# A filter layer with tokens on partitions, and another order in the experts' first pass

## The chip, the cores and the metric

One NeuronCore of a Trainium2 chip runs the whole kernel. It has five engines that work side by side: TensorE (PE; PEld are its weight loads), VectorE (DVE), ScalarE (ACT), GpSimd (POOL) and SyncE (SP), which only issues DMAs here. An engine works through its own instructions in order and waits on semaphores for the others. The metric is the device time of one execution in microseconds; lower is better.

## The reference

The input x has 2 sequences of 1024 tokens with 128 features, 2048 tokens in all, in f32. Four layers are added to it one after the other: A, F, B, F (A is a gated recurrent layer; the change does not touch it).

- B, the filter layer, on n = layernorm(x): q, k, v = n Wq', n Wk', n Wv'; each is Fourier transformed along its 128 features to 65 complex numbers; fq and fk are divided by (magnitude + 1e-8); fkv = running sum over the tokens of a sequence of fk * fv; the result is the inverse transform of fkv * conj(fq), and the layer returns n plus it. So x becomes x + n + values.
- F, on layernorm(x): causal attention with 16 heads, then four expert networks of which each token takes the best two by a softmax over four router logits. Expert 1 is silu(h W1) * (h W2), then a down product. Experts 0, 2 and 3 have one, three and two hidden layers with gelu. The first 32 output features of attention and experts are set to zero.

## The kernel before

X holds the tokens on partitions, as 16 tiles of 128 tokens by 128 features. Work goes in 4 chunks of 512 tokens (`NCH`, `TPC` = 4 tiles a chunk); chunks 0 and 1 are the first sequence. Every engine's program is written out by hand, and the order of a function's lines is the order on that engine's queue. PSUM is eight banks of 512 f32 (`PS`), handed out in turn by `Banks.take`; `psum_full` counts results written there, `psum_read` results copied away, and `all_read` waits for all.

**Filter layer (`b_tensor`, `b_scalar`, `b_vector`, `b_gpsimd`, lines 987 to 1162).** TensorE multiplies each of the three weights with the DFT table (L996); ScalarE copies the products to `bwf` (L1039), takes the root for the layernorm and copies the transposed normed tokens to HT (L465). Then `spectra(c)` makes, for a chunk, spectra with frequencies on 65 partitions and 512 tokens along the row (L1006): real and imaginary part of q, k, v, six banks. ScalarE squares q and k out of PSUM (L1045), copies all three (L1052), and takes the root of the squares' sums (L421). VectorE sums the squares (L1068), adds epsilon (L1074), takes the reciprocal (L1075) and scales q and k by it (L1079): this is `unit(c)`. GpSimd multiplies k and v (`b_times`, L1131 to L1133). VectorE makes the running sums along the row with two scans a chunk (L1090), the second half of a sequence carrying on from the first. GpSimd multiplies by conj(q) (`b_unbind`, L1144 to L1148). TensorE transforms back (L1018), which puts tokens on partitions again; VectorE adds it to X (`add`, L1097) and takes the layernorm's statistics for the next layer (`stats`, L410 and L413). For the last chunk VectorE does `b_times` and `b_unbind` itself. The first transposes and four QKV products (L447) of the next F layer stand between the last `output` calls on TensorE.

**Experts (end of `f_tensor`, `f_scalar`, `f_vector`).** When a sequence's last heads are added up (`heads_added`), TensorE projects its attention output (`proj`, L1333), VectorE joins it to XL (`join`), and the normed result is transposed to HT. The first pass is expert 1: two `up` products a chunk (L1386), `silu(c)` on ScalarE (L1544), `gate(c)` on VectorE (L1732), and `down1(c)` (L1407), whose result VectorE adds with the token's weight (`add1`, L1770). The weights come from the router product (L1440, 32 records of 4 columns), a softmax and a chain of small comparisons on VectorE (L1741 to L1765). The second pass goes over the chunks with experts 0, 2 and 3: `up`, `mid` (L1397), `down` (L1417), gelu on ScalarE (L1562). `down1(c)` for c of 2 and 3 waits until `add1(c-2)` has freed its bank. Chunks 0 and 1 of the first pass start while the second sequence's projection is still outstanding.

**Weights.** `w_sync` on SP's queue, in layer A, loads the weights of B and F with eleven DMAs; `W_LOADED` is the count that their users wait for.

Of the kernel before, what the change touches and what calls it, by code (L numbers as in the profile page):

```python
# [16 lines left out]
P = 128  # L17
B, S, D = 2, 1024, 128
NT = B * S
# [73 lines left out]
def hybrid_kernel(nc, x, a_w, a_wab, a_small, a_conv, a_bog, a_bout, a_wout, b_w, b_dft, b_idft,  # L93
                  f_w, f_n, f_qk, f_mid, f_down, f_wo, f_rows, eye, causal, out):
    ctx = ExitStack()
    with ctx:
# [108 lines left out]
        with ExitStack() as sw:  # L205
# [3 lines left out]
            bidft = sb("bidft", [P, 2, D], at=sw, side="right")  # L209
            bwf = sb("bwf", [P, 3, 2, NB], at=sw, side="right")  # L210
# [13 lines left out]
            with ExitStack() as sB:  # L224
                QF = {i: sb(f"QF{i}", [P, 3, 2, CH], at=sB) for i in (1, 2, 0)}
                KV = [sb(f"KV{i}", [P, 4, CH], at=sB) for i in range(2)]
                SQF = sb("SQF", [P, 2, 2, CH], at=sB)
                mag = [sb(f"mag{i}", [P, 2, CH], at=sB) for i in range(2)]
                PRB = sb("PRB", [P, 4, CH], at=sB)
                CUM = sb("CUM", [P, 2, B, S], at=sB)  # L230
                YF = sb("YF", [P, 2, NT], at=sB)
# [94 lines left out]
        sums_ready = sem("sums_ready")  # L326
# [660 lines left out]
        B_RES = 3 + NCH + 3 * NCH  # L987
        OUT_BANKS = 6

        def b_tensor(pe, banks, nth):  # L990
            base = banks.n
            pe.wait_ge(w_loaded, W_LOADED)
            pe.wait_ge(x_ready, nth)
            for n in range(3):
                k = banks.take()
                pe.matmul(PS[:, k, 0:2 * NB], bw[:, n, :], bdft[:].rearrange("p r f -> p (r f)"),  # L996
                          start=True, stop=True).then_inc(psum_full, 1)
            pe_transpose_in(pe, banks, XL, FIRST_NORM[nth])
            banks.all_read()

            def spectra(c):
                for n in range(3):
                    if c:
                        pe.wait_ge(psum_read, banks.n - 2)
                    for r in range(2):
                        last = pe.matmul(PS[0:NB, 2 * n + r, :], bwf[:, n, r, :], HT[:, c * CH:(c + 1) * CH],  # L1006
                                         start=True, stop=True)
                    last.then_inc(psum_full, 1)
                    banks.n += 1

            def output(c):
                pe.wait_ge(y_ready, c + 1)
                if c >= 2:
                    pe.wait_ge(values_added, c - 1)
                for i in range(TPC):
                    t = (c * TPC + i) * P
                    for r in range(2):
                        last = pe.matmul(PS[:, OUT_BANKS + c % 2, i * P:(i + 1) * P], YF[0:NB, r, t:t + P],  # L1018
                                         bidft[0:NB, r, :], start=(r == 0), stop=(r == 1))
# [4 lines left out]
            for c in range(NCH // B):  # L1024
                output(c)
            assert banks.n == base + B_RES
            banks.all_read()
            for g in range(NCH // B):
                pe.wait_ge(values_added, g + 1)
                pe_transpose_x(pe, banks, g)  # L1030
            output(NCH - 2)
            for t in range(TPC):
                pe_qkv(pe, banks, FIRST_RESULT[nth + 1], t)
            output(NCH - 1)

        def b_scalar(act, link, ask, reads):
            for n in range(3):
                k = reads.next()
                act.activation(bwf[:, n].rearrange("p r f -> p (r f)"), PS[:, k, 0:2 * NB],  # L1039
                               ACT.Copy).then_inc(psum_read, 1)  # L1040
            act_sqrt(act, ask, stat[:])
            act_ht(act, reads)
            for c in range(NCH):
                act.wait_ge(psum_full, reads.n + 2)
                act.activation(SQF[0:NB], PS[0:NB, 0:4, :].rearrange("p (n r) t -> p n r t", n=2),  # L1045
                               ACT.Square).then_inc(squares_ready, 1)
                if c >= 3:
                    act_sqrt(act, ask, mag[c % 2][0:NB])
                    act.wait_ge(y_ready, c - 2)
                for n in range(3):  # L1050
                    reads.next()
                    act.activation(QF[c % 3][0:NB, n], PS[0:NB, 2 * n:2 * n + 2, :], ACT.Copy).then_inc(psum_read, 1)  # L1052
# [881 lines left out]
```

## Time and profile before

| | us |
|---|---|
| median of 3 runs (1143.45 to 1147.26) | 1146.95 |
| the profiled execution | 1147.34 |
| its span, first to last instruction | 1145.5 |
| busy: PE, DVE, ACT, POOL | 678.0, 830.2, 534.1, 328.0 |

The mean granted clock of TensorE is 0.775 of full speed (1.0 is 2.4 GHz, 0.5 is 1.2 GHz). Busy shares are means over layers with different limits, so a layer is read by itself: first a row of its stretch with each engine's busy time, then the chain of work that ended last in it, then the groups and the single instructions. In such rows x is the number of instructions, and brackets give the idle time before an instruction and what ended it. Times are us from the span's start unless marked ns; a matmul record is one pass, and an f32 product leaves two.

### The profile page before, as it was taken

The page shows a single profiled execution, that of the slowest core. Times are in us where ns is not written, and L with a number is a line of the kernel's source. Part 1 is how long each engine was busy: PE and PEld are TensorE (multiplying, and loading weights), DVE is VectorE, ACT ScalarE, POOL GpSimd, SP SyncE. Part 2 cuts the span into 40 slices and gives each one's busy share as a digit, 9 for nine tenths or more (in the row PEclk, how much of TensorE's full clock was granted, in tenths as well). Part 3 has the DMA queues.
Part 4 walks back from the last instruction along what each step waited for, and adds up shares of the span by engine and source line. Part 5 has one row for each costly group of instructions (what it writes and reads, how often), then busy time and mean ns, then how long its engine had stood idle before and what let it go on. Part 6 is the DMA issues. An engine that isn't in the chain of part 4 may idle for free.

```text
span 1145.5 us, 11993 instructions
## 1 busy us (share of the span) xinstructions
PE 678.0 (59%) x4000; PEld 327.8 (29%) x4000; DVE 830.2 (72%) x1478; ACT 534.1 (47%) x882; POOL 328.0 (29%) x290
## 2 busy tenths in 40 slices
PE   3993004000004007598888889873275988879998
PEld 1452004000003005222222556530251222225555
DVE  5899999888889997966586523359989665865212
ACT  2414003333331004699998322252146999983222
POOL 1050652000003303257655000006812576550000
PEclk9985555555555557599999889977575999998999
DMA  3150048400000010541010000000005311100000
GB/s 96 60 157 4 3 101 180 132 19 19 0 19 19 0 27 10 178 130 57 29 57 1 1 1 1 1 1 0 0 1 185 122 57 31 55 1 1 1 19 19
DMA packets 37253, 51.30 MB, mean 45 GB/s; under 512 B 5128, under 2 KB 27016, under 8 KB 36168
## 3 DMA queue, kind: packets, MB, share of 16 engines
q1 hardware_dynamic: 36424, 49.76, 15.8%
q10 hardware_dynamic: 768, 0.79, 0.4%
q8 instruction: 32, 0.52, 0.2%
q14 instruction: 29, 0.24, 0.1%
HBM read 21.02 MB, written 16.92 MB: 33 GB/s over the span
## 4 chain that ended last, share of the span: by engine, by line
DVE 44%; PE 24%; POOL 11%; ACT 9%; issue 8%; DMA 2%; SPq 1%; ACTq 1%; DVEq 0%; POOLq 0%
POOL PX L1284 10%; PE PS L1397 6%; ACT PX L1537 6%; PE PS L1386 5%; PE PS L1417 4%; DVE S L847 4%; DVE D L843 4%; DVE P L844 3%; DVE P L840 3%; DVE mag L1075 2%; PE PS L1372 2%; DVE RP L862 2%; DVE PRR L861 2%; DVE CUM L1090 1%; PE PS L1407 1%
## 5 line engine op out<-in xcount | busy, mean ns | idle before, releaser
L1537 ACT ACTIVATE PX<-PS 128x1024 f32<-128x1024 f32 (+1 forms) x320 | 270.9, 975 | 13.3 <-PE PS L1352 12.9
L1284 POOL TENSOR_TENSOR PX<-PX,maskf 128x256 f32<-128x256 f32 (+1 forms) x192 | 178.0, 961 | 118.1 <-ACT PX L1537 118.1
L1372 PE MATMUL PS<-PX,VA 128*32 128x512 f32 (+3 forms) x1536 | 166.7, 505 | 27.8 <-POOL PX L1284 18.2
L1770 DVE SCALAR_TENSOR_TENSOR X<-PS,wts,X 128x96 f32<-128x96 f32 x128 | 38.4, 315 | 121.0 <-PE PS L1417 103.9
L1352 PE MATMUL PS<-QS,KS 64*128 64x512 bf16 (+3 forms) x768 | 105.5, 339 | 7.5 <-ACT PX L1537 4.4
L1709 DVE RECIPROCAL DEN<-DEN 128x512 f32<-128x512 f32 x32 | 107.3, 3353 | 1.1
L611 PE MATMUL PS<-fw,ones 128*128 128x384 f32 x2 | 1.6, 928 | 160.1 <-DVE fw L1567 160.1
L718 ACT ACTIVATE P<-S,AC 128x16 f32<-128x16 f32 x128 | 41.2, 322 | 114.4 <-DVE S L847 114.4
L983 POOL TENSOR_TENSOR PRQ<-PA,LQK 128x2048 f32<-128x2048 f32 (+7 forms) x8 | 20.8, 2616 | 200.4 <-DMA WS<-S 183.2
L1386 PE MATMUL PS<-HT,fw 128*128 128x512 f32 x144 | 72.8, 656 | 1.5 <-DVE HG L1732 1.0
L1352 PEld LDWEIGHTS PS<-QS,KS 64*128 64x128 bf16 x768 | 30.1, 94 | 140.7 <-ACT PX L1537 83.5
L606 PE MATMUL PS<-ones,HT 64*128 64x1 f32 x64 | 13.0, 348 | 90.4 <-ACT HT L702 90.4
L1372 PEld LDWEIGHTS PS<-PX,VA 128*32 128x32 f32 x1536 | 33.0, 108 | 81.4 <-ACT PX L1537 53.3
L1131 POOL TENSOR_TENSOR KV<-QF 65x1024 f32<-65x1024 f32 x3 | 9.1, 3041 | 161.3 <-DVE QF L1079 159.0
L1707 DVE LOAD_MASK_SELECT DEN<-PS x32 | 0.4, 14 | 73.0 <-PE PS L1372 71.5
L465 ACT ACTIVATE HT<-PS 128x512 f32<-128x512 f32 x24 | 13.8, 600 | 79.1 <-PE PS L438 57.1
L611 PEld LDWEIGHTS PS<-fw,ones 128*128 128x128 f32 x2 | 0.5, 310 | 160.2 <-DVE fw L1567 160.2
L843 DVE TENSOR_REDUCE D<-P 128x16 f32<-128x144 f32 x128 | 38.8, 303 | 5.2 <-ACT P L711 0.7
L847 DVE TENSOR_REDUCE S<-P 128x16 f32<-128x144 f32 x128 | 38.8, 303 | 4.6 <-DVE P L844 0.2
L586 PE MATMUL PS<-HT,CWT 128*128 128x512 f32 (+3 forms) x96 | 41.4, 593 | 0.0
L840 DVE TENSOR_TENSOR P<-W,S 128x128 f32<-128x128 f32 x128 | 37.3, 292 | 4.6
L629 PE MATMUL PS<-awout,RT 128*128 128x128 f32 x32 | 6.6, 402 | 57.4 <-DMA RT<-RO 57.4
(276 smaller groups left out, 1532.9 us busy)
## 6 DMA issues: line engine op xcount, KB each, us to landing
QS<-qs_d SPq DMA_DIRECT2D x64, 98.0 KB
qs_d<-QP SPq DMA_DIRECT2D x24, 256.0 KB, 3.6
ks_d<-QP SPq DMA_DIRECT2D x24, 256.0 KB, 3.9
KS<-ks_d SPq DMA_DIRECT2D x64, 96.0 KB
K<-LQK SPq DMA_DIRECT2D x16, 256.0 KB
W<-WS SPq DMA_DIRECT2D x16, 256.0 KB, 4.4
qkv_d<-CY SPq DMA_DIRECT2D x3, 1024.0 KB, 4.0
LQK<-qkv_d SPq DMA_DIRECT2D x8, 256.0 KB, 4.9
```

The source lines that it names most:

```text
L586: last = pe.matmul(PS[:, k, skip:CH], CWT[:, 4 * n + j, :], HT[:, t + skip - back:t + CH - back], start=(j == 3), stop=True, skip_group_ch ...
L840: link(v.tensor_tensor(P1[:, n % 2, :, :, 0:HD], bcast(W2[:, g, cs], 1, 2), bcast(S2[:, n], 2, C), ALU.mult))
L843: link(v.tensor_reduce(D2[:, g, :, cs], P1[:, n % 2], AX.X, ALU.add))
L847: v.tensor_reduce(S2[:, n + 1], P2[:], AX.X, ALU.add).then_inc(chunk_done, 1)
L1284: pool.tensor_tensor(block, block, bcast(maskf[:], 1, 2 * halves), ALU.mult).then_inc(probs_masked, 1)
L1352: last = pe.matmul(PS[:, 2 * (u % DEPTH) + side, at:at + CH - c0], KS[b][rows, pair, kt * P:(kt + 1) * P], QS[b][rows, pair, qc * CH + c0: ...
L1372: last = pe.matmul(PS[32 * h:32 * h + 32, SCORES_BANKS + qc, c0:CH], VA[b][:, kt, h, :], px[:, i % 2, at:at + CH - c0], start=(kt == 0), s ...
L1386: last = pe.matmul(PS[:, bank + m, :], fw[:, col + m * P:col + (m + 1) * P], rhs(c), start=True, stop=True)
L1397: last = pe.matmul(PS[:, bank + m, :], fmid[:, w + k, m * P:(m + 1) * P], h, start=(k == 0), stop=(k == len(parts) - 1))
L1417: last = pe.matmul(PS[:, 6 + t % 2, j * OUTC:(j + 1) * OUTC], h[:, m, t * P:(t + 1) * P], fdown[:, e, m, :], start=(m == 0), stop=(m == 1))
L1537: act.activation(tile(PX[u % PDEPTH][:]), tile(PS[:, k:k + 2, :]), ACT.Exp).then_inc(probs_ready, 1)
L1709: v.reciprocal(DEN[:], DEN[:]).then_inc(den_ready, 1)
```

## The change

**Filter layer.** Tokens now stay on the partitions. `bwf` becomes one row of 3x2x65 columns, and `spectra(c)` takes HT's tile as the stationary side and `bwf` as the moving one: per tile of 128 tokens 390 numbers, in banks 4 to 7, handed over two tiles at a time. The frequencies are stored rotated by one, so that frequency 0 comes last. ScalarE squares and copies by pairs of tiles. The running sum becomes TensorE products (`sums`): a triangular matrix (`maskf`) for the tile itself, a matrix of ones for the tiles before it in the chunk, and `LAST`, which picks the last token's row, for the carry from the chunk before. ScalarE copies the sums (`CUM`), in its program ahead of the root of the chunk two later. `b_unbind` makes products only; `turn` transposes and adds them with products against identity and minus identity (`NIDENT`), ScalarE copies the result, and `output` is one product a tile, since its 128 rows now hold the 65 real and 63 imaginary parts. Buffers are one per chunk, with fewer waits between chunks. VectorE writes three constant tiles into SQ. The weights-by-DFT products wait for the first F layer's last expert addition in place of the layer's statistics; `bidft` is loaded by three DMAs. For the last chunk VectorE unbinds straight from PSUM and copies the turned tile.

**Experts, both F layers.** `up(0, 2)` and `up(1, 0)` go ahead of the wait for the last heads and the projections of chunks 2 and 3. The ups of chunks 2 and 3 go ahead of the router's product, `silu(2)` and `silu(3)` ahead of the router's exponential, `gate(2)` and `gate(3)` ahead of the router's work on VectorE. `down1(2)` and `down1(3)` go behind the last `mid` of the second pass's chunk 0.

```diff
-        B_RES = 3 + NCH + 3 * NCH
-        OUT_BANKS = 6
+        B_RES = 3 + NCH + 2 * NCH
+        SPEC_BANK, SUM_BANK, TURN_BANK = 4, 0, 2
+        OUT_BANK = (3, 7, 3, 3)
...
-            pe.wait_ge(x_ready, nth)
+            pe.wait_ge(down_read, 2 * TILES)
             for n in range(3):
                 k = banks.take()
                 pe.matmul(PS[:, k, 0:2 * NB], bw[:, n, :], bdft[:].rearrange("p r f -> p (r f)"),
                           start=True, stop=True).then_inc(psum_full, 1)
+            pe.wait_ge(x_ready, nth)
             pe_transpose_in(pe, banks, XL, FIRST_NORM[nth])
-            banks.all_read()
...
+                for p in range(2):
+                    pe.wait_ge(psum_read, banks.n - 1 if c else base + 3 + 1)
+                    for i in range(2 * p, 2 * p + 2):
+                        t = (c * TPC + i) * P
+                        last = pe.matmul(PS[:, SPEC_BANK + i, 0:3 * 2 * NB], HT[:, t:t + P], bwf[:],
                                          start=True, stop=True)
                     last.then_inc(psum_full, 1)
...
+            def sums(c):
+
+                pe.wait_ge(kv_ready, c + 1)
+                pe.wait_ge(sums_read, c)
+                carry = c % (S // CH) > 0
+                for i in range(0, TPC, 2):
+                    two, second = SUMS_PS[:, i:i + 2], SUMS_PS[:, i + 1]
+                    if carry:
+                        pe.matmul(two, LAST, bcast(CUM[c - 1][:, TPC - 1], 1, 2), start=True, stop=False,
+                                  skip_group_check=True)
+                    for j in range(i):
+                        pe.matmul(two, ONES, bcast(KV[c][:, j], 1, 2), start=(j == 0 and not carry), stop=False,
+                                  skip_group_check=True)
+                    pe.matmul(two, maskf[:], KV[c][:, i:i + 2], start=(i == 0 and not carry), stop=False,
+                              skip_group_check=True)
+                    last = pe.matmul(second, ONES, KV[c][:, i], start=False, stop=True, skip_group_check=True)
+                last.then_inc(sums_full, 1)
+
+            def turn(c):
+
+                pe.wait_ge(y_ready, c + 1)
+                pe.wait_ge(turned_ready, c)
+                for i in range(TPC):
+                    at = slice(i * P, (i + 1) * P)
+                    pe.matmul(PS[:, TURN_BANK, at], ABF[c][:, 0, i, 0:P], ident[:], start=True, stop=False,
+                              skip_group_check=True)
+                    pe.matmul(PS[0:P // 2, TURN_BANK, at], ABF[c][:, 1, i, 0:P // 2], ident[:], start=False, stop=True,
+                              skip_group_check=True)
+                    last = pe.matmul(PS[P // 2:P, TURN_BANK, at], ABF[c][:, 1, i, P // 2:P], NIDENT, start=False,
+                                     stop=True, skip_group_check=True)
+                last.then_inc(turned_full, 1)
...
+            sums(0)
+            sums(1)
+            turn(0)
+            output(0)
+            sums(2)
+            turn(1)
             banks.all_read()
+            output(1)
+            sums(3)
+            turn(2)
             for g in range(NCH // B):
                 pe.wait_ge(values_added, g + 1)
                 pe_transpose_x(pe, banks, g)
-            output(NCH - 2)
+            output(2)
+            turn(3)
             for t in range(TPC):
                 pe_qkv(pe, banks, FIRST_RESULT[nth + 1], t)
-            output(NCH - 1)
+            output(3)
...
             for c in range(NCH):
...
+                spectra(c)
+                if c >= 2:
+                    sums(c - 2)
+                act_sqrt(act, ask, mag[c][:])
+            turned(0)
+            sums(2)
+            turned(1)
+            turned(2)
...
+        def b_times(eng, link, c):
+
+            k = QKF[c][:].rearrange("p (t n) r f -> p t n r f", n=2)[:, :, 1]
+            w, to = VF[c], TKV[c]
+            out = KV[c][:].rearrange("p t (r f) -> p t r f", r=2)
+            link.open(eng.tensor_tensor(to[:, 0], k, w[:], ALU.mult))
+            link.open(eng.tensor_tensor(to[:, 1, :, 0], k[:, :, 0], w[:, :, 1], ALU.mult))
+            link(eng.tensor_tensor(to[:, 1, :, 1], k[:, :, 1], w[:, :, 0], ALU.mult))
+            eng.tensor_tensor(out[:, :, 0], to[:, 0, :, 0], to[:, 0, :, 1], ALU.subtract)
+            if c == NCH - 1:
+                eng.wait_ge(kv_ready, NCH - 1)
+            eng.tensor_tensor(out[:, :, 1], to[:, 1, :, 0], to[:, 1, :, 1], ALU.add).then_inc(kv_ready, 1)
...
             pe.wait_ge(psum_read, banks.n - 1)
             up(0, 0, F_E1A)
             banks.all_read()
+            up(0, 2, F_E1B)
+            pe.wait_ge(up_read, hidden + 1)
+            up(1, 0, F_E1A)
             pe.wait_ge(heads_added, (rep * B + 2) * (NG - 1) * 2)
             for c in range(NCH // B, NCH):
                 proj(c, HT_BANKS + c - NCH // B)
-            up(0, 2, F_E1B)
-            pe.wait_ge(up_read, hidden + 1)
-            up(1, 0, F_E1A)
             pe.wait_ge(h1_ready, gated + 1)
             up(1, 2, F_E1B)
             down1(0)
             pe_transpose_in(pe, banks, SQ, FIRST_NORM[nth], range(NCH // B, NCH), HT_BANKS - NCH // B)
             down1(1)
             banks.all_read()
+            for c in range(NCH // B, NCH):
+                pe.wait_ge(up_read, hidden + c)
+                up(c, 0, F_E1A)
+                pe.wait_ge(h1_ready, gated + c)
+                up(c, 2, F_E1B)
...
                 mid(4, 2, [HB[:, k, :] for k in range(2)])
+                if c == 0:
+                    down1(NCH - 2)
+                    down1(NCH - 1)
...
-            for dst, src in ((bw, b_w), (bdft, b_dft), (bidft, b_idft), (fw, f_w), (fn, f_n), (fmid, f_mid),
+            for dst, src in ((bidft[0:NB - 1], b_idft[1:NB, 0]), (bidft[NB - 1:NB], b_idft[0:1, 0]),
+                             (bidft[NB:P], b_idft[1:P - NB + 1, 1])):
+                sp.dma_start(dst, src).then_inc(w_loaded, 16)
...
+            silu(2)
+            silu(3)
             ask.wait()
             act.activation(pr[:], lg[:], ACT.Exp).then_inc(to_dve, 1)
-            silu(2)
-            silu(3)
...
             v.tensor_tensor(X[:], X[:], XL[:], ALU.add).then_inc(x_sum, 1)
+            gate(2)
+            gate(3)
```

## Rows read from the trace of the kernel before

**Rows 1.** Stretches of the filter layer: length, busy us by engine (records), clock, DMA.
```profile
766.70:820.90 54.20, 18.77 (x46) 7.57 (x44) 53.92 (x20) 16.87 (x15) 35.54 (x19) 0.68 0.00 0
820.90:848.40 27.50, 15.79 (x68) 13.11 (x68) 24.38 (x43) 4.75 (x11) 11.06 (x6) 0.57 0.00 0
```

**Rows 2.** Stretches of the first expert layer, same view.
```profile
647.40:657.40 10.00, 10.00 (x17) 3.83 (x16) 5.05 (x24) 4.24 (x5) 0.00 (x0) 0.71 0.00 1
657.40:665.10 7.70, 3.50 (x17) 3.51 (x17) 5.65 (x24) 0.63 (x1) 0.00 (x0) 0.68 0.01 2
...
680.70:743.70 63.00, 60.79 (x283) 38.72 (x281) 19.00 (x72) 17.85 (x19) 0.00 (x0) 1.00 0.00 1
```

**Rows 3.** Chain of waits, filter layer: shares by engine, tile, line.
```profile
by line: DVE mag L1075 25.1%; DVE CUM L1090 15.6%; DVE QF L1079 10.0%; issue 6.4%; PE PS L1006 5.1%; DVE mag L1074 4.3%; DVE XL L417 4.0%; PE PS L447 3.6%; PE PS L1018 3.3%; ACT QF L1052 2.6%; DVE mag L1068 2.4%; PE PS L432 1.9%; ACT SQF L1
```

**Rows 4.** Line L1709: count, ns min/median/max, first and last start, form.
```profile
L1709 DVE RECIPROCAL DEN<-DEN x32: 3352/3353/3354, 491.5 to 1026.0; 128x512 f32<-128x512 f32 x32
```

**Rows 5.** Groups in the filter layer by form: busy us, mean ns, idle before.
```profile
L1075 DVE RECIPROCAL mag<-mag 65x1024 f32<-65x1024 f32 x4 | 26.2, 6549 | 0.1
...
L465 ACT ACTIVATE HT<-PS 128x512 f32<-128x512 f32 x7 | 4.2, 598 | 36.9 <-PE PS L438 32.1 <-PE PS L432 4.8
...
L1097 DVE TENSOR_TENSOR X<-X,PS 128x512 f32<-128x512 f32 x4 | 2.7, 666 | 0.0
...
L1144 DVE TENSOR_TENSOR PRB<-CUM,QF 65x1024 f32<-65x1024 f32 x1 | 1.2, 1222 | 0.0
```

**Rows 6.** Timeline of the filter layer: start, us, engine, line, [idle before].
```profile
745.22 1.42 PE L996 MATMUL PS<-bdft,bw 128*128 128x130 f32 x6 [2.57 <-issue]
...
763.90 5.37 PE L1006 MATMUL PS<-HT,bwf 128*65 128x512 f32 x12 [1.16 <-ACT QF L1052]
...
777.30 0.68 DVE L1074 TENSOR_SCALAR mag<-mag 65x1024 f32<-65x1024 f32 x1
...
780.15 1.27 POOL L1132 TENSOR_TENSOR KV<-QF 65x512 f32<-65x512 f32 x1
...
791.26 2.17 POOL L1132 TENSOR_TENSOR KV<-QF 65x512 f32<-65x512 f32 x1
792.30 1.68 DVE L1074 TENSOR_SCALAR mag<-mag 65x1024 f32<-65x1024 f32 x1
...
837.29 3.62 PE L1018 MATMUL PS<-bidft,YF 65*128 65x128 f32 x16
...
845.14 1.95 PE L1018 MATMUL PS<-bidft,YF 65*128 65x128 f32 x16
```

**Rows 7.** Line L1567, columns as in rows 4.
```profile
L1567 DVE TENSOR_SCALAR fw<-fw,fn x1: 412/412/412, 358.1 to 358.1; 128x384 f32<-128x384 f32 x1
```

**Rows 8.** Timeline of the first expert layer, columns as in rows 6.
```profile
630.67 2.00 PE L1333 MATMUL PS<-fwo,AO 128*128 128x96 f32 x16 [2.32 <-DVE AO L1715]
...
635.89 1.22 DVE L1732 TENSOR_TENSOR HG<-HS,PS 128x1024 f32<-128x1024 f32 x1
...
643.38 4.06 PE L1440 MATMUL PS<-fw,HT 128*128 128x4 f32 x32
...
647.30 10.12 PE L1386 MATMUL PS<-HT,fw 128*128 128x512 f32 x16
...
661.62 3.70 PE L1407 MATMUL PS<-fdown,HG 128*128 128x96 f32 x16 [4.20 <-DVE X L1770]
```

**Rows 9.** Stretches cut finer, for the granted clock, same view as rows 1.
```profile
788.00:804.00 16.00, 0.56 (x2) 0.56 (x3) 15.93 (x7) 2.31 (x3) 15.20 (x8) 0.56 0.00 0
...
844.00:848.00 4.00, 3.53 (x24) 2.77 (x22) 1.74 (x3) 2.13 (x6) 0.00 (x0) 0.95 0.00 0
...
660.00:664.00 4.00, 2.38 (x11) 2.41 (x12) 3.43 (x11) 0.00 (x0) 0.00 (x0) 0.52 0.00 0
1031.00:1036.00 5.00, 5.00 (x20) 3.67 (x21) 2.81 (x4) 0.00 (x0) 0.00 (x0) 0.66 0.01 3
```

**Rows 10.** Stretch of the second expert layer, same view as rows 1.
```profile
1064.30:1080.20 15.90, 15.90 (x49) 8.16 (x48) 1.98 (x8) 4.58 (x5) 0.00 (x0) 0.94 0.00 1
```

More of the change, by code:

```diff
@@ L1011, in output @@
             def output(c):
-                pe.wait_ge(y_ready, c + 1)
+                pe.wait_ge(turned_ready, c + 1)
                 if c >= 2:
-                    pe.wait_ge(values_added, c - 1)
+                    pe.wait_ge(values_added, 1 if c == 2 else c)
                 for i in range(TPC):
[L1016 to L1019, printed above, removed]
+                    at = slice(i * P, (i + 1) * P)
+                    last = pe.matmul(PS[:, OUT_BANK[c], at], YT[c][:, at], bidft[:], start=True, stop=True)
@@ L1023, in b_tensor @@
                 spectra(c)
-            for c in range(NCH // B):
-                output(c)
             assert banks.n == base + B_RES
+            pe.wait_ge(consts_ready, 1)
+            sums(0)
[4 more added lines that the diff above has]
+            turn(1)
             banks.all_read()
+            output(1)
+            sums(3)
+            turn(2)
             for g in range(NCH // B):
@@ new lines, in sums, with turned @@
+            def sums(c):
+                act.wait_ge(sums_full, c + 1)
+                act.activation(CUM[c][:], SUMS_PS, ACT.Copy).then_inc(sums_read, 1)
+            def turned(c):
+                act.wait_ge(turned_full, c + 1)
+                act.activation(YT[c][:], PS[:, TURN_BANK, :], ACT.Copy).then_inc(turned_ready, 1)
+            for c in range(NCH):
+                spectra(c)
+                if c >= 2:
+                    sums(c - 2)
+                act_sqrt(act, ask, mag[c][:])
@@ L1104, in b_vector @@
             sum_squares(0)
-            unit(0)
-            for c in range(1, NCH):
+            for c in range(NCH):
                 unit(c)
-                sums(c - 1)
-                if c >= 3:
-                    add(c - 3)
-                    stats(c - 3)
             v.wait_ge(unit_ready, NCH)
-            v.wait_ge(sums_ready, NCH - 2)
-            link(b_times(v, NCH - 1))
-            sums(NCH - 1)
-            add(NCH - 3)
-            stats(NCH - 3)
-            b_unbind(v, link, NCH - 1)
@@ new lines, in b_unbind @@
+        def b_unbind(eng, c, sums):
+            q = QKF[c][:].rearrange("p (t n) r f -> p t n r f", n=2)[:, :, 0]
+            z = sums.rearrange("p t (r f) -> p t r f", r=2)
+            to = ABF[c][:].rearrange("p w t (r f) -> p w t r f", r=2)
+            eng.tensor_tensor(to[:, 0], z, bcast(q[:, :, 0], 2, 2), ALU.mult)
+            eng.tensor_tensor(to[:, 1, :, 0], z[:, :, 1], q[:, :, 1], ALU.mult)
+            eng.tensor_tensor(to[:, 1, :, 1], z[:, :, 0], q[:, :, 1], ALU.mult).then_inc(y_ready, 1)
@@ L1443, in f_tensor @@
             assert banks.n == base + F_RES
-            for c in range(NCH // B, NCH):
-                pe.wait_ge(up_read, hidden + c)
-                up(c, 0, F_E1A)
-                pe.wait_ge(h1_ready, gated + c)
-                up(c, 2, F_E1B)
-            down1(NCH - 2)
             pe.wait_ge(up_read, hidden + NCH)
@@ L1752, in f_vector @@
             for i in range(E4):
-                if i == 2:
-                    gate(2)
                 for j in range(i):
@@ L1778, in add1 @@
                     add_expert(c * TPC + t, 1, PS[:, 6 + c % 2, t * OUTC:(t + 1) * OUTC]).then_inc(down_read, 1)
-            add1(0)
-            gate(3)
-            for c in range(1, NCH):
+            for c in range(NCH):
                 add1(c)
```

151 lines of the change are left out of this document (70 added, 81 removed).

## The prediction

> **What bounds the kernel now.** I read the stages first: each row is one stretch's length, busy time by engine and granted clock. In the filter layer's loop, 54.2 us, VectorE is busy 53.92 and TensorE 18.77; in its last 27.5 us VectorE 24.38 [rows 1]. The layer runs from the last expert addition, 743.7, to its own last addition, 848.4: 104.7 us. In the experts [rows 2] TensorE has the most work, but does 10.00 us of first-pass products at a clock of 0.71 and is busy only 3.50 of the 7.70 us behind them. From 680.7 on it is busy 60.79 of 63.0; that stretch is at its bound and the change leaves it alone. The chain of waits in the filter layer [rows 3] says what ends last: reciprocals 25.1%, scans 15.6% (16 us), scaling of q and k 10.0%, all VectorE. Groups and timeline give prices and order.
>
> The profiled execution took 1147.34 us, span 1145.5; the median of the runs is 1146.95. I sum against 1147.3, 0.03% off.
>
> **The filter layer, price by price.** The spectra go from 65 partitions to 128: a chunk of 512 tokens becomes 4 tiles by 130 numbers for each of q, k, v.
>
> VectorE. Reciprocal: 520 in a row instead of 1024. 512 cost 3.353 [rows 4], 1024 cost 6.549 [rows 5], so 520 cost 3.40; 3.15 saved, four times. Squares' sum: 520, by L1097's 512 in 0.67, so 0.68. Scaling: 1040, by L1144's 1024 in 1.22, so 1.24 [rows 5]. Epsilon: half of L1074's 0.68, so 0.4. The scans go to TensorE. While GpSimd works the short steps stretch: L1074 took 1.68 beside L1132's 2.17, 0.68 alone [rows 6]. I take 1.35 times; the ends 1.0 and 1.7 are worth 2.6 us less and 2.6 more over the layer.
>
> GpSimd. Products of a chunk: 520 + 4x260 numbers; L1132's 512 took 1.27 alone, 2.17 beside VectorE [rows 6], so 1.3 + 4x0.7 = 4.1 to 7; I take 5.0. Unbinding, 520 + 2x260: 2.75.
>
> ScalarE. Two squares of 520, two pairs of copies, a root; by L465's 512 in 0.60 [rows 5] 0.61 each and 0.9 a pair, 3.6 a chunk, below VectorE's 6.2.
>
> TensorE. Each f32 product leaves two records. One of 128 columns takes 0.122 us at the high clock, 0.23 at the low (L1018: 16 in 1.95 and 3.62); one of 512 takes 0.45 (L1006: 12 in 5.37) [rows 6]. So at the high clock spectra, 390 columns, are 1.3 per two tiles; sums, four products of 260 and two of 130, 2.2, with a carry two more of 260, 3.1; turning, 24 records, 2.9; output, 8 records, 1.0. All nearly double at the low clock.
>
> **Schedule at these prices.** *Front.* The weights-by-DFT products wait for the last expert addition, 743.75, and no longer for the statistics: L996 starts 1.4 us earlier than 745.22 [rows 6]. Two tiles instead of a chunk suffice for the first square. First reciprocal 762.3, not 767.4: 5.1 saved. *Loop.* Four units of epsilon 0.54, reciprocal 3.40, squares' sum 0.75, scaling 1.6 make 24.5 us. A wait is added: ScalarE copies chunk c-2's sums ahead of chunk c's root, so behind it are queued root 2 and with it all of VectorE's unit 2. Sums 0 need GpSimd's products of chunk 0 (773.2) and TensorE past its last spectra (772.0). I expect some 8 us at the low clock here, as TensorE has 2.6 us of work in each 6; sums 0 end 777.6, root 2 at 778.9, and VectorE, free at 774.6, loses 4.3. Loop ends 791.0, not 820.9: 24.8 more saved. *Tail.* Sums 2 from 790.4 to 792.6, copy, turn 1 to 796.1, copy, output 1 to 797.8, sums 3 to 800.9, turn 2 to 803.9, transposes of two chunks 1.3, output 2 to 806.3, turn 3 to 809.2, four QKV tiles (384 columns each) to 811.8, their copies and the squares' sums of q and k, together 3.6 by estimate and in the old tail too, last addition 816.1. That is 25.1 against 27.5: 2.4 saved, TensorE-bound where VectorE and GpSimd were. Together 848.4 - 816.1 = 32.3; what follows hangs on this addition as before.
>
> The three constant tiles (about 0.7 of VectorE) lie under the first spectra. bidft's load becomes three DMAs ahead of the other weights, two issues more on SP; the first weight is used at 358.1 [rows 7], some 150 us after its issue, so even 10 us would be covered.
>
> **The experts, price by price.** Now TensorE idles 2.3 us for the last heads, then projects at 630.67 and goes on with up products; gate 0 runs at 635.89 [rows 8]. After: two up products (3.5) go ahead of that wait, fill it, and push the projections to 631.85. Joins, squares and gate 0 behind them come 1.2 later (gate 0 ends 638.3), and TensorE, with nothing left, idles 633.7 to 638.3. The idle 4.2 before L1407 at 661.62 was followed by a clock of 0.52 [rows 8, 9], so a fall here is likely (1.9 lost). Then nothing interrupts: up 1.75, down 1.9, transposes 1.05, down 1.9, four ups 7.0, to 651.9 (653.8 with the fall). Router 3.95 by L1440, its read 0.5, second pass from 656.4 (658.3) instead of 665.1. Now the 16 records after the router take 10.12 us [rows 8] where the high clock needs 7; that low stretch moves onto the second pass, 2.5 lost again (1.7 to 3.4). The gap of 4.2 goes, and so does L1407's low-clock 3.70. Inside the second pass's chunk 0 two down products (3.6) replace one. The choice of experts, some 38 VectorE steps of about 0.2, 6.8 us by estimate, ends near 665; the down products that need its additions come at 672. That hides it; with the cover gone each late us is a us. Chunk 1 starts 675.3 (677.2), not 680.7: 5.4 (3.5) saved. In the second expert layer the projections begin at 1031.0 and chunk 1 at 1080.2 [rows 9, 10], 49.2 against 50.0, so 4.5 (2.7). Together 6.2 to 9.9; I take 7.5.
>
> **Sum:** 1147.3 - 32.3 - 7.5 = 1107.5.
>
> **Rivals.** *Low clock through the filter layer.* TensorE's work comes in pieces between waits; from 788 to 804 the clock was 0.56 [rows 9], and the L1018 burst at 837 still ran low [rows 6]. Low from 765 to 800 the addition ends at 823, total 1114; low to the end, 30 us of TensorE's tail become 60 and it ends at 844, total 1135. Against: from 784 on TensorE has work almost without a gap, and the burst from 836 on had brought 0.95 by 844 to 848 [rows 9]. The Trainium skill (TensorE: Matmul & The Clock Gate, "A second HAM failure mode: psum-queue depth-cycling") has such micro-idles make the clock oscillate, which would be this rival; no run of this order shows it yet.
> *VectorE held by GpSimd.* If each of eight short steps in units 1 to 3 waited out a whole GpSimd instruction of 1.3, they would lose 10.4 instead of 2.6: 1115; half of one on average, 1110. For: L1074, issued at 792.30, ends at 793.98, about its lone 0.68 after L1132 ended at 793.43. Against: the reciprocal kept its 6.55 throughout, and it is over half of a unit, so many steps will meet a GpSimd engine between instructions. The Trainium skill (SBUF — State Buffer, "Who interferes with whom") makes it an exclusive lock for the whole instruction; the row agrees.
> *High clock and no contention:* addition at 810, experts 10: 1099.
> *The experts give nothing:* pause at 633.7 and the moved low stretch eat it all: 1115.
> *Slower: weight loads not hidden.* Sums, turns and outputs have 184 records, each with a 128-wide load. L1407's records, 96 columns, took 0.23 each at the low clock, so a load costs no more. Were each to stand before its stream, 42 us come on top of 60, addition at 886, total 1177; it decides once the tail needs over 72 us. Against: L1018 gets through load and stream of 128 columns in that same 0.23.
>
> **How the numbers follow.** Forecast 0.54; low clock 0.14; VectorE held 0.10; high clock 0.10; experts nothing 0.08; slower 0.03; saved so little that it can't be told 0.01. Under 0.5%, 5.7 us, can't be told from no change. The filter layer's 25 to 37 and the experts' 2 to 12 give 1098 to 1120; with part of the low-clock case 1096 to 1123. Faster 0.95 (all but the last two, less a hundredth for a low clock with more against it), same 0.02, slower 0.03.
>
> **What would show it.** Right: reciprocals near 3.4; root 2 waiting for sums 0; some 72 us from the experts' last addition to the filter layer's; a pause of 4 to 5 us before gate 0 and none before chunk 2's down products. Wrong: a clock near 0.5 after 790, short VectorE steps over twice their lone price, a second pass that still waits at its start, or attention stretches that change.

## The result and the profile after

The changed kernel took 1100.18 us (median; 1098.63 to 1102.87) against 1145.20 (1142.39 to 1147.26) for the kernel before, run beside it: ratio 0.9612, 95% interval 0.9592 to 0.9632. Its profiled execution took 1101.15, span 1099.0: 46.5 less span than before. I forecast 1107.5.

I take the account between marks that both traces have. From the last head addition of attention to the last expert addition: 113.2 before, 109.3 after in the first expert layer, 3.9 saved. From there to the filter layer's last addition: 104.7 and 65.2, 39.5 saved. From the second attention's last head addition to the end of the span: 114.65 and 112.27, 2.4 saved. From the filter layer's last addition to the first exponential of the next attention it is 32.7 before and 32.9 after. What is left, 0.7, lies in stretches that the change does not touch.

Stretches of the changed kernel: the filter layer's loop and its tail, then the first expert layer up to its second chunk, and the rest of it (length, busy us of TensorE, its weight loads, VectorE, ScalarE, GpSimd with records; granted clock; DMA).

```profile
754.90:781.80 26.90, 20.25 (x92) 14.15 (x91) 22.29 (x16) 11.36 (x24) 16.45 (x21) 0.94 0.00 1
781.80:803.70 21.90, 19.36 (x135) 14.15 (x133) 13.39 (x40) 6.21 (x14) 3.12 (x3) 1.00 0.00 1
629.20:636.70 7.50, 3.04 (x19) 2.16 (x18) 4.90 (x8) 2.51 (x3) 0.00 (x0) 0.83 0.01 2
636.70:645.00 8.30, 8.26 (x45) 6.19 (x45) 4.75 (x4) 1.99 (x3) 0.00 (x0) 0.75 0.00 0
645.00:656.60 11.60, 11.27 (x50) 7.35 (x48) 2.70 (x4) 3.71 (x4) 0.00 (x0) 0.91 0.00 0
656.60:675.60 19.00, 18.92 (x63) 10.38 (x64) 9.20 (x48) 7.14 (x8) 0.00 (x0) 0.87 0.00 1
675.60:738.50 62.90, 60.71 (x283) 38.66 (x282) 19.96 (x76) 16.81 (x18) 0.00 (x0) 1.00 0.00 1
```

Against [rows 1]: the loop is 26.9 where it was 54.2, VectorE no longer fills it (22.29), and TensorE works 20.25 in it. In the tail TensorE is busy 19.36 of 21.9 at the high level (1.00) where the old tail had 0.57. Against [rows 2]: the 62.9 us at the end of the experts stand as they were; the gain lies ahead of them.

The chain of waits in the filter layer, shares by line:

```profile
by line: DVE mag L1148 10.5%; PE PS L1047 9.0%; PE PS L1049 8.7%; DVE XL L426 6.4%; PE PS L1018 5.7%; PE PS L1034 5.0%; PE PS L1061 4.9%; PE PS L1036 4.7%; PE PS L1031 3.8%; DVE QKF L1152 3.5%; issue 3.1%; PE PS L441 3.0%; PE PS L1038 2.4%;
```

In [rows 3] three VectorE lines led it. Now the reciprocal is 10.5%, and of the next eight lines seven are TensorE: the layer has changed its bound. In order of time the chain still runs through VectorE's first two units up to 766, then through GpSimd's products of chunk 1 to 770, and from there through TensorE and the copies that it waits for. How much each part of the new layer brings is read from this; no run takes one part alone.

Groups of the layer (busy us, mean ns) and its timeline (start, us, engine, line, idle before):

```profile
L1148 DVE RECIPROCAL mag<-mag 128x520 f32<-128x520 f32 x4 | 13.6, 3402 | 0.1
...
L1152 DVE TENSOR_TENSOR QKF<-QKF,mag 128x1040 f32<-128x1040 f32 x4 | 4.9, 1236 | 0.0
```

```profile
752.42 0.70 DVE L1141 TENSOR_TENSOR mag<-SQF 128x520 f32<-128x520 f32 x1 [3.39 <-ACT SQF L1100]
...
754.95 3.40 DVE L1148 RECIPROCAL mag<-mag 128x520 f32<-128x520 f32 x1
...
765.31 1.04 PE L1034 MATMUL PS<-KV,SQ 128*128 128x260 f32 x4
...
768.21 0.64 DVE L1147 TENSOR_SCALAR mag<-mag 128x520 f32<-128x520 f32 x1 [2.23 <-ACT mag L430]
...
770.03 0.71 PE L1031 MATMUL PS<-CUM,SQ 128*128 128x260 f32 x2 [3.01 <-POOL KV L1196]
...
772.69 1.70 PE L1034 MATMUL PS<-KV,SQ 128*128 128x260 f32 x4
...
776.25 0.79 DVE L1147 TENSOR_SCALAR mag<-mag 128x520 f32<-128x520 f32 x1 [2.07 <-ACT mag L430]
...
780.52 1.24 DVE L1152 TENSOR_TENSOR QKF<-QKF,mag 128x1040 f32<-128x1040 f32 x1
...
797.78 2.85 PE L456 MATMUL PS<-fw,HT 128*128 128x384 f32 x8
...
803.04 0.68 DVE L1157 TENSOR_TENSOR X<-X,PS 128x512 f32<-128x512 f32 x1
```

The reciprocal measures the 3.40 that [rows 4, 5] gave. VectorE waits twice for a root that stands behind a copy of sums, as forecast for one of them. Four records of 260 columns (two products) cost 1.04 at 765.31 and 1.70 at 772.69, behind TensorE's wait of 3.01. The granted clock by stretches of 4 us, around this wait and at the start of the experts' second pass:

```profile
766.00:770.00 4.00, 1.02 (x6) 0.73 (x4) 1.75 (x2) 2.95 (x7) 3.85 (x6) 1.00 0.02 6
770.00:774.00 4.00, 3.97 (x12) 3.24 (x13) 3.96 (x3) 0.72 (x2) 2.43 (x3) 0.58 0.00 0
774.00:778.00 4.00, 4.00 (x30) 2.68 (x28) 1.89 (x3) 1.13 (x2) 3.66 (x5) 1.00 0.00 0
...
655.00:659.00 4.00, 3.59 (x9) 2.36 (x10) 2.09 (x12) 1.54 (x2) 0.00 (x0) 0.50 0.01 2
```

In this execution the clock is high while TensorE waits, low when it starts again, and high 4 us on.

TensorE's timeline in the first expert layer after, with the gate that it waits for:

```profile
635.47 1.22 DVE L1793 TENSOR_TENSOR HG<-HS,PS 128x1024 f32<-128x1024 f32 x1
...
636.74 3.78 PE L1447 MATMUL PS<-HT,fw 128*128 128x512 f32 x4 [4.50 <-DVE HG L1793]
640.31 2.21 PE L1468 MATMUL PS<-fdown,HG 128*128 128x96 f32 x16
...
644.99 7.06 PE L1447 MATMUL PS<-HT,fw 128*128 128x512 f32 x16
651.89 4.39 PE L1506 MATMUL PS<-fw,HT 128*128 128x4 f32 x32
656.68 6.86 PE L1447 MATMUL PS<-HT,fw 128*128 128x512 f32 x10 [0.41 <-DVE lg L1804]
```

The wait of 4.20 of [rows 8] is gone; one of 4.50 has come ahead of gate 0, with four records at 3.78 behind it, which take 1.98 at the high clock (the same four in two of the runs below). The ten records after the router take 6.86; ten of the 16 in 7.06 are 4.4.

### The profile page after: what moved, and what is told of

Read it like the earlier page. It is cut to its first block, busy times and chain, and to the rows that moved or that the text cites. A ratio compares the mean times of both kernels' runs of the same rounds, so it can differ in the third digit from the quotient of the medians.

```text
span 1099.0 us, 12216 instructions
## 1 busy us (share of the span) xinstructions
PE 672.6 (61%) x4104; PEld 331.8 (30%) x4104; DVE 788.6 (72%) x1474; ACT 527.7 (48%) x899; POOL 299.6 (27%) x290
## 4 chain that ended last, share of the span: by engine, by line
DVE 39%; PE 28%; POOL 12%; ACT 8%; issue 8%; DMA 3%; SPq 2%; ACTq 1%; DVEq 0%; POOLq 0%
POOL PX L1345 11%; PE PS L1447 7%; PE PS L1458 6%; ACT PX L1598 6%; PE PS L1478 4%; DVE D L852 4%; DVE S L856 4%; DVE P L853 4%; DVE P L849 3%; PE PS L1433 2%; DVE RP L871 2%; DVE PRR L870 2%; PE PS L1468 1%; PE PS L1413 1%; SPq L1274 1%
## 5 line engine op out<-in xcount | busy, mean ns | idle before, releaser
L1433 PEld LDWEIGHTS PS<-PX,VA 128*32 128x32 f32 x1536 | 32.9, 108 | 80.2 <-ACT PX L1598 53.4
L1447 PEld LDWEIGHTS PS<-HT,fw 128*128 128x128 f32 x144 | 29.6, 212 | 45.1 <-issue 31.4
L1190 POOL TENSOR_TENSOR TKV<-QKF,VF 128x520 f32<-128x520 f32 x3 | 3.7, 1233 | 141.3 <-DVE QKF L1152 141.3
```

The costliest lines, as they stand in the source:

```text
L1433: last = pe.matmul(PS[32 * h:32 * h + 32, SCORES_BANKS + qc, c0:CH], VA[b][:, kt, h, :], px[:, i % 2, at:at + CH - c0], start=(kt == 0), s ...
L1447: last = pe.matmul(PS[:, bank + m, :], fw[:, col + m * P:col + (m + 1) * P], rhs(c), start=True, stop=True)
```

## The experiments

**The changed kernel again**, no edit, beside the next two.

> The changed kernel once more, as a base for the runs beside it. Both theories: about 1100 us, 0.961 of the kernel before.

1101.06 (1098.76 to 1103.12), ratio 0.9614 [0.9593, 0.9635]. Its stretches repeat: 109.8, 64.9, 112.5. One thing differs: sums 1 start 30.0 us after the last expert addition and take 6.1 until the first turning starts, where the first profile has 31.5 and 4.9, so the clock is low there for longer:

```profile
770.00:774.00 4.00, 4.00 (x10) 3.26 (x11) 3.97 (x3) 0.66 (x2) 2.37 (x3) 0.50 0.00 0
774.00:778.00 4.00, 4.00 (x23) 2.88 (x23) 0.71 (x2) 1.13 (x2) 3.72 (x6) 0.76 0.00 0
```

The layer ends at the same place either way, but a run with an edit must be held against the profile with the same low stretch.

**Each half alone.** The filter layer with the experts' old order, and the reverse (all functions of the filter layer as before):

```diff
-            for c in range(NCH // B, NCH):
-                pe.wait_ge(up_read, hidden + c)
-                up(c, 0, F_E1A)
-                pe.wait_ge(h1_ready, gated + c)
-                up(c, 2, F_E1B)
...
             last.then_inc(psum_full, 1)
...
+            for c in range(NCH // B, NCH):
+                pe.wait_ge(up_read, hidden + c)
+                up(c, 0, F_E1A)
+                pe.wait_ge(h1_ready, gated + c)
+                up(c, 2, F_E1B)
+            down1(NCH - 2)
```

```diff
-                        last = pe.matmul(PS[:, SPEC_BANK + i, 0:3 * 2 * NB], HT[:, t:t + P], bwf[:],
...
+                        last = pe.matmul(PS[0:NB, 2 * n + r, :], bwf[:, n, r, :], HT[:, c * CH:(c + 1) * CH],
```

> The filter layer's part alone, the experts as before. Theory, by the two traces: the layer went from 104.7 to 65.2 us (743.71 to 848.4 and 738.53 to 803.7), so 39.5 of the gain are its own and this takes about 1106. Rival, that the two parts need each other (the clock that the experts leave behind, buffers): the filter part alone gives 32 or less, the 32.3 of the forecast, and this takes 1113 or more.

> The experts' new order alone, the filter layer as before. Theory, by the two traces: from the last heads to chunk 1 of the second pass 50.2 became 46.4 in the first expert layer and 49.3 about 47 in the second, so 6 us: about 1139. Rival, that the pause before gate 0 and the moved low clock eat it: within 2 us of 1145. Forecast's middle: 7.5, about 1138.

filter_only: 1106.96 (1106.43 to 1107.16), ratio 0.9665 [0.9649, 0.9682]; filter layer 64.9, first experts 113.2 as before. experts_only: 1139.28 (1136.31 to 1142.03), ratio 0.9955 [0.9937, 0.9972]; 109.8 and 104.7. Alone they save 38.0 and 5.7 against their runs of before (1145.0), 43.8 in sum; together they save 43.9 against the same runs. They add; neither needs the other.

**Which of the new order's moves costs?** Chunk 0's second pair and chunk 1's first pair of products behind the projections again, the rest of the change kept:

```diff
-            up(0, 2, F_E1B)
-            pe.wait_ge(up_read, hidden + 1)
-            up(1, 0, F_E1A)
...
+            up(0, 2, F_E1B)
+            pe.wait_ge(up_read, hidden + 1)
+            up(1, 0, F_E1A)
             pe.wait_ge(h1_ready, gated + 1)
```

> The changed kernel with the two up products back behind the projections; the rest of the experts' new order stays. Theory (the pause costs): gate 0 comes 1.2 us earlier, TensorE's wait for it shrinks from 4.5 to about 1 us, the low clock behind it (two products in 3.78 where 1.75 is the full price) goes: 2 to 3 us saved per expert layer, 4 to 6 in all, about 1095. Rival (what is ahead is won): the 3.5 us of up products are back on the path, 2 to 3 us lost per layer, about 1105.

1094.52 (1094.36 to 1096.51), ratio 0.9564 [0.9547, 0.9581]: 6.5 below after_again. Putting products ahead of the projections, which I had priced as filling the wait, lost 3 us in each layer: the stretches are 106.4 and 108.9, where the changed kernel has 109.3 and 112.3. TensorE's timeline in the first layer:

```profile
629.58 2.79 PE L1394 MATMUL PS<-fwo,AO 128*128 128x96 f32 x16 [2.32 <-DVE AO L1776]
632.16 4.53 PE L1447 MATMUL PS<-HT,fw 128*128 128x512 f32 x8
636.87 1.98 PE L1447 MATMUL PS<-HT,fw 128*128 128x512 f32 x4 [0.17 <-DVE HG L1793]
...
654.75 6.07 PE L1447 MATMUL PS<-HT,fw 128*128 128x512 f32 x10 [0.41 <-DVE lg L1804]
```

The heads' wait of 2.32 is back, but the 4.50 ahead of gate 0 is 0.17, and the records behind it are at 1.98. They hardly start earlier, though: 7.4 us after the last head addition, against 7.5 in the changed kernel, because the projections (2.79) and the eight records (4.53) ran low. In the second layer these took 2.00 and 3.62 behind the same wait, and the start is at 6.6. So in the first layer all that was gained is clock, not the earlier gate that the theory named.

**One pair ahead, one behind**, the split of the two:

```diff
             up(0, 2, F_E1B)
-            pe.wait_ge(up_read, hidden + 1)
-            up(1, 0, F_E1A)
...
+            pe.wait_ge(up_read, hidden + 1)
+            up(1, 0, F_E1A)
```

> The changed kernel with one up product (chunk 0's second) ahead of the wait for the last heads and the other behind the projections. Theory: it fills the 2.3 us in which TensorE waited for the heads without pushing the projections back, gate 0 stays at its early place and the wait for it is still covered by the other product: about 1094.5, as with both behind, or 1 to 2 us less. Rival (any product ahead delays gate 0): between 1095 and 1100.

1092.95 (1089.48 to 1094.51), ratio 0.9544 [0.9521, 0.9567]. In its profile the first expert layer took 103.2, the second stretch 108.8; the profiled execution was the fastest of its four (1089.48), so these two are its best and not its middle.

**Is it the clock and not the wait?** Four products of no use (8 records) between the projections and the wait for gate 0; order as in the change:

```diff
+            for i in range(4):
+                pe.matmul(PS[:, 7, :], fw[:, 0:P], HT[:, 0:CH], start=True, stop=True)
             pe.wait_ge(h1_ready, gated + 1)
```

> The changed kernel, with four products of 512 columns put on TensorE behind the projections whose results nobody reads (bank 7, overwritten later), so that it works through 3.5 of the 4.5 us in which it waits for gate 0. Theory (the low clock after the pause is part of the cost): the two products behind gate 0 take 2.0 and not 3.8, 1.5 to 2 us saved per expert layer, 3 to 4 in all, about 1097. Rival (only the late gate 0 costs, the clock is hidden): within 1 us of 1100.

1092.61 (1089.52 to 1093.06), ratio 0.9539 [0.9518, 0.9560]: 7.6 below the changed kernel's 1100.18, more than was expected. TensorE's timeline in the first layer, and one line of the second:

```profile
637.99 1.98 PE L1447 MATMUL PS<-HT,fw 128*128 128x512 f32 x4 [1.03 <-DVE HG L1795]
...
651.10 3.63 PE L1508 MATMUL PS<-fw,HT 128*128 128x4 f32 x32
655.13 4.53 PE L1447 MATMUL PS<-HT,fw 128*128 128x512 f32 x10 [0.41 <-DVE lg L1806]
...
1006.93 6.23 PE L1447 MATMUL PS<-HT,fw 128*128 128x512 f32 x10 [0.41 <-DVE lg L1806]
```

The added 3.6 us lie in the wait. Behind it 1.98 stands for 3.78, and, unforeseen, the router takes 3.63, not 4.39, and the second pass's start 4.53, not 6.86; in the second layer it takes 6.23, not 7.31. The records behind gate 0 start 7.51 after the last head addition, to the hundredth as in the changed kernel: gate 0 is no earlier, only the clock differs. Work that computes nothing saved 7.6 us, so the low clock was the loss.

**The router in two lots among the pass**, so that no 32 small records stand in a row:

```diff
                 up(c, 0, F_E1A)
+                last = router(range((c - 2) * TB, (c - 1) * TB))
                 pe.wait_ge(h1_ready, gated + c)
                 up(c, 2, F_E1B)
...
-            for t in range(TILES):
-                last = pe.matmul(PS[:, ROUTER_BANK, t * E4:(t + 1) * E4], HT[:, t * P:(t + 1) * P],
```

> The changed kernel with the router's 32 small records split in two and put between the up products of chunks 2 and 3, instead of in one piece behind them; nothing else. Theory (the router's piece is what lets the clock fall at the start of the second pass, 6.86 us for 10 records where 4.5 is the full price, and leaves a wait of 0.4): 2 to 2.8 us saved per layer, 4 to 5.5 in all, about 1095.5. Rival (the fall comes from the pause before gate 0 and the low stretch behind it, or moves to another place): within 1.5 us of 1100.

1095.48 (1094.31 to 1099.30), ratio 0.9567 [0.9540, 0.9593]. The ten records take 4.53 in both layers (and in both of best and best2 below, which have the router in lots too; behind the router in one piece they take 4.53 only in the first layer of one_ahead and of filler, and 6 us or more in every other profile). The wait ahead of them grew from 0.41 to 1.59, since on VectorE the read now stands behind a gate; the 3.78 after gate 0 stays. Its slowest run reaches into the changed kernel's range.

**Is the wait for the root on the path?** A chunk's root ahead of the copy of sums on ScalarE:

```diff
                 spectra(c)
+                act_sqrt(act, ask, mag[c][:])
                 if c >= 2:
                     sums(c - 2)
-                act_sqrt(act, ask, mag[c][:])
```

> The changed kernel, with ScalarE taking the root of chunk c before it copies the sums of chunk c-2. VectorE's two waits of 2.2 and 2.1 us before units 2 and 3 go. Theory (the layer is bound by TensorE from the sums of chunk 1 on, 770 to 798, and by unit 1 and GpSimd's products before them): at most 1 us saved, 1099 to 1101. Rival (VectorE's loop still sets the end, as the forecast had it): 4 us saved, about 1096.

1103.17 (1099.52 to 1103.81), ratio 0.9631 [0.9609, 0.9653]. VectorE's last scaling there:

```profile
777.91 1.36 DVE L1152 TENSOR_TENSOR QKF<-QKF,mag 128x1040 f32<-128x1040 f32 x1
```

It ends 38.4 after the last expert addition (740.86) instead of 43.2, and the layer still takes 65.0; after_again, with the same start (30.0) and length (6.1) of sums 1, takes 64.9. Nearly 5 us taken from VectorE's loop are worth nothing: its end is off the path. The total is 2 to 3 us above the changed kernel's and not within the forecast 1099 to 1101; no stretch that the edit touches shows a loss.

**Half of the turning left out**, two of three products a tile:

```diff
-                    pe.matmul(PS[0:P // 2, TURN_BANK, at], ABF[c][:, 1, i, 0:P // 2], ident[:], start=False, stop=True,
...
-                    last = pe.matmul(PS[P // 2:P, TURN_BANK, at], ABF[c][:, 1, i, P // 2:P], NIDENT, start=False,
...
```

> The changed kernel without the second half of the turning (the two 64-row products a tile against identity and minus identity are left out, so the imaginary parts' share of the values is missing). They take 0.35 us a tile on TensorE, 1.4 a chunk. Theory (TensorE bounds the layer's second half): 4 to 5.6 us saved, about 1095.5. Rival (copies, GpSimd and VectorE are next and hide it): under 2 us, 1098 or more.

1100.03 (1092.07 to 1100.60), ratio 0.9596 [0.9569, 0.9622]: the total did not fall. The layer takes 62.7, 2.3 to 2.5 less where 4 to 5.6 were expected. Its clock, and TensorE at sums 3:

```profile
770.00:774.00 4.00, 3.83 (x10) 3.17 (x11) 3.96 (x3) 0.86 (x3) 2.57 (x4) 0.50 0.00 0
...
786.00:790.00 4.00, 2.62 (x7) 2.24 (x8) 2.48 (x5) 0.00 (x0) 0.23 (x1) 0.54 0.00 0
790.00:794.00 4.00, 4.00 (x16) 3.26 (x16) 0.43 (x1) 0.00 (x0) 0.00 (x0) 0.61 0.00 0
```

```profile
787.38 1.24 PE L1031 MATMUL PS<-CUM,SQ 128*128 128x260 f32 x2 [3.12 <-DVE KV L1191]
```

The first low stretch stands ahead of any turning and is that of after_again (sums 1 take 6.1). With less to do TensorE then waits 3.12 ahead of sums 3 for VectorE's products of chunk 3, which are next in line, and the clock is low a second time, from 786, where the changed kernel has 1.00: sums 3 take 6.0 us and not 3.1. So of the work left out a part comes back as a wait for VectorE, a part as work at half speed. Five of its six runs lie from 1099.8 to 1100.6; the sixth, 1092.07, has no profile and stays unexplained.

**Products of chunk 1 on VectorE** instead of GpSimd, to take away TensorE's wait of 3.01:

```diff
             for c in range(NCH):
                 unit(c)
+                if c == 1:
+                    v.wait_ge(unit_ready, 2)
+                    b_times(v, link, 1)
...
-            for c in range(1, NCH - 1):
-                times(c)
-                unbind(c - 1)
-            unbind(NCH - 2)
+            unbind(0)
+            times(2)
+            unbind(1)
+            unbind(2)
```

> The changed kernel with chunk 1's products of k and v on VectorE, which waits 2.2 us there for root 2, instead of GpSimd's 4.0 us. Theory: the sums of chunk 1 start at 768.5 and not 770.0, TensorE's idle stretch before them shrinks from 3 to 1.5 and the low clock behind it (3.1 us of sums in 5.0) goes, but the sums of chunk 2 then wait for GpSimd's products of chunk 2 near 778.5, so the layer gains 1 to 1.5 us only: 1099. Rival (the layer's length is TensorE's chain from 770 on, one for one): 3 to 3.5 us saved, 1097.

1100.61 (1099.06 to 1102.87), ratio 0.9607 [0.9583, 0.9631]; the layer takes 66.85, 1.7 more: a miss. Its timeline says why:

```profile
769.52 0.71 PE L1031 MATMUL PS<-CUM,SQ 128*128 128x260 f32 x2 [2.25 <-DVE KV L1199]
...
770.34 3.40 DVE L1148 RECIPROCAL mag<-mag 128x520 f32<-128x520 f32 x1
...
780.84 1.69 POOL L1207 TENSOR_TENSOR ABF<-CUM,QKF 128x260 f32<-128x260 f32 x1
...
783.70 0.49 PE L1047 MATMUL PS<-ident,ABF 128*128 128x128 f32 x2 [1.44 <-POOL ABF L1208]
```

TensorE's wait shrank only to 2.25, the low clock behind it stays (sums 1 take 4.9 as before), the reciprocal of chunk 2 starts 1.2 later counted from the last expert addition, GpSimd's products 2 and its unbinding of chunk 1 move back with it, meet VectorE's products (1.69 for a step of 0.69) and hold up turn 1.

**Together.** best is one_ahead, router_mixed and products1_vector; best2 is the first two, with two products of no use ahead of the wait for gate 0:

```diff
+            for i in range(2):
+                pe.matmul(PS[:, 7, :], fw[:, 0:P], HT[:, 0:CH], start=True, stop=True)
```

> The changed kernel with three edits: one up product ahead of the wait for the heads and one behind the projections, the router's records between the up products, chunk 1's products on VectorE. Theory: 1100.5 - 8 - 3 (the router's low stretch, where it was left) - 1 = 1088 to 1090. Rival (each edit gives the same low clock back): 1092 or more.

> Chunk 1's first pair of products behind the projections, the router's products in two lots among the pass, and two products without use (512 columns each, into a free bank) ahead of the wait for gate 1; the filter layer as in the changed kernel. Theory (the savings add where each removes a stretch at the low clock): the order alone gave 7.5 us (1100.5 to 1093.0) and the router in lots 5.0 (1100.5 to 1095.5), but the first of these already shortens the second expert layer, so 1089 to 1091. Rival (the clock gives back elsewhere in the layer what a removed pause saves): no better than the order alone, 1092.5 or more.

best: 1093.69 (1092.48 to 1095.12), ratio 0.9545 [0.9523, 0.9567], a miss: its filter layer takes 66.2, so products1_vector costs here as it does alone. best2: 1091.54 (1090.08 to 1092.44), ratio 0.9537 [0.9518, 0.9556], half a us past what the theory gave and not told apart from one_ahead or filler. The second expert layer of one_ahead, then of best2, then one line of best:

```profile
985.05 1.98 PE L1447 MATMUL PS<-HT,fw 128*128 128x512 f32 x4 [2.75 <-DVE HG L1793]
...
1002.96 6.85 PE L1447 MATMUL PS<-HT,fw 128*128 128x512 f32 x10 [0.41 <-DVE lg L1804]
```

```profile
988.90 1.98 PE L1447 MATMUL PS<-HT,fw 128*128 128x512 f32 x4 [1.03 <-DVE HG L1800]
...
1007.35 4.53 PE L1447 MATMUL PS<-HT,fw 128*128 128x512 f32 x10 [1.60 <-DVE lg L1811]
```

```profile
990.30 2.79 PE L1450 MATMUL PS<-HT,fw 128*128 128x512 f32 x4 [2.75 <-DVE HG L1801]
```

Between one_ahead and best2 the lots bought 2.3 for 1.2 of wait here. In the first layer of one_ahead's profile the ten records took 4.53 already, so there the lots only cost: in that execution this is why the savings do not add. Behind one and the same wait of 2.75 the four records took 1.98 in one_ahead and 2.79 in best. Both, and proj_first, one_ahead and filler, lie clear of both kernels; router_mixed does by its median.

## Why the prediction was right, and which term was mis-sized

**The mechanism held in the main**: the filter layer passes from VectorE to TensorE, the parts add (38.0 and 5.7 alone), what follows hangs on the layer's last addition as before. Of the signs named, reciprocals at 3.40, root 2 behind sums 0, a pause of 4.50 before gate 0 and none before chunk 2's down products came. The 72 us did not: the layer takes 65.2. That is the mis-sized term. It saved 7.2 us more than forecast, while the experts saved 1.2 less.

**Filter layer: 32.3 forecast, 39.5 measured.** *Front* 5.1, measured 7.3: the first reciprocal came 16.4 after the last expert addition, not 18.6. The trace takes this apart. The squares' sum, which stood here before,

```profile
763.04 1.22 DVE L1068 TENSOR_TENSOR mag<-SQF 65x1024 f32<-65x1024 f32 x1 [7.71 <-ACT SQF L1045]
```

starts 5.4 earlier than it did (13.9 after that addition, not 19.3); that is the forecast's 5.1. The other 1.8 lie between its start and the reciprocal's, 2.5 for 4.3: sum, root and epsilon have half the row, and the root stands 0.7 and not 1.3 behind copies. I had priced the shorter steps in the loop; the front's working names none of them. *Loop* 24.8, measured 26.7: the waits for roots came to 4.3 as forecast, but at two roots (2.23 and 2.07); VectorE's steps took 22.3, not 24.5 (the four units as listed add up to 25.2, or 24.6 from the first reciprocal on). My 1.35 for GpSimd beside it, which I had given in full to the epsilon step alone, was too dear: the scaling kept 1.24, as GpSimd had run out of work when it began, and its products of a chunk took 4.0, not 5.0. *Tail* 2.4, measured 5.5. Sums 2 ended 0.3 behind the loop, not 1.6, and from QKV's end to the last addition's end went 3.1, not 4.3: the copies run beside QKV. So most of the small prices were taken on the dear side, and they pointed one way. One step of the path was wrong: the forecast led it through all four of VectorE's units, with the wait for root 2 in it. root_first shows that this wait, though it came, was off the path; the chain of waits leaves VectorE after unit 1 and passes through GpSimd's products of chunk 1 into TensorE's wait of 3.01.

**The low clock in the layer** was forecast, 8 us of it, at sums 0; it came at sums 1, for 3 to 4 us in the first profile (0.58 over 4 us), and for longer in after_again. The rival *low clock through the filter layer* did not come: 1.00 from 774 on. turn_half shows that it was near: with less work the clock was 0.54 at 786. The Trainium skill (TensorE: Matmul & The Clock Gate, "A second HAM failure mode: psum-queue depth-cycling"), which I had set beside this rival, has short waits make the clock swing; the trace has one swing, 1.00, 0.58, 1.00 from 766 to 778, behind a single wait of 3.01, and none in the 20 us behind it, where TensorE waits 0.70 and 0.79 for copies.

**Experts: 7.5 forecast, 6.3 measured**, and 6.2 was the sum with both falls of the clock. Each step is there: a pause of 4.50 (4.6 forecast), the fall behind it (3.78 for 1.98, so 1.8; 1.9 forecast), the low stretch moved onto the second pass (6.86 and 7.31 for 4.5; 2.5 forecast), the choice of experts covered by the second pass. I should have taken 6.2: the rows of before showed a low clock behind both a like wait and the router. What I did not see is that filling the heads' wait with products was itself a loss, of 6.5 us in all; the experiments show that keeping one pair back, or even adding useless work, gets it back.

**The other rivals.** *VectorE held by GpSimd*: epsilon steps of 0.42 took up to 0.79, but all of VectorE's steps in the loop together 22.3; no. *Weight loads not hidden*: in the tail's 21.9 us lie 19.36 of records and 14.15 of loads, so the loads ran beside them; no. *High clock, no contention*, 1099, is nearest in time, but the experts' half of it did not come, nor a loop at the high clock throughout.

**Left open**: what decides the clock behind the router, since in one_ahead the same 32 records were followed by 4.53 in the first layer and 6.85 in the second, and behind waits of 2.3 to 2.8, which either level followed; and the single run at 1092.07.

## What to carry to other kernels

When work moves to an engine whose clock has two levels in the trace, price each stretch behind a wait at both, and spread the work that is at hand over the coming waits rather than using it all up at the first: one pair of products kept back was worth more than the wait that it had filled. Before shortening a wait, look whose chain ends last behind it; VectorE's loop got 5 us shorter here for nothing. Before giving an edit a difference of 1 or 2 us, see whether the unchanged kernel shows it too from run to run. Small unknown prices that are all taken on the dear side add up to a bias, 7 us here.

## What the runs showed of the hardware that I had not expected

Products of no use made the kernel 7.6 us faster, and leaving out 5.6 us of work shortened its layer by 2.5 at most, both with a change of the granted clock. The two half-width products of turning (64 output rows each) start within 0.01 of each other, pair by pair. That bought nothing against the forecast: from one tile's start to the next it is 0.79, and six records at its 0.122 make 0.73, so a chunk's turning took 3.1 us where 2.9 were forecast.

```profile
776.37 0.49 PE L1047 MATMUL PS<-ident,ABF 128*128 128x128 f32 x2
776.78 0.32 PE L1049 MATMUL PS<-ident,ABF 128*64 128x128 f32 x1
776.79 0.32 PE L1051 MATMUL PS<-SQ,ABF 128*64 128x128 f32 x1
...
777.15 0.49 PE L1047 MATMUL PS<-ident,ABF 128*128 128x128 f32 x2
```
